# Edge stages of a four-layer graph kernel: ten numbers per quad read in one load of bytes

## The reference

```python
# L0, two layers          # L1                              # L3, two layers
msg = x[src] * ew         messages = x[col] @ W_msg + b     h_ref = x[src] - 2 * dot * rel[etype]
agg = segment_sum(msg, dst)  msg_sum = segment_sum(messages, row)   out = segment_sum(h_ref, tgt)
```

## Time and profile before

| | |
|---|---|
| runs | 4398.54, 4406.31, 4406.6 us; median 4406.31 us |
| span of the profiled execution | 4783.9 us |
| TensorE clock granted, mean | 0.898 |
| PE busy | 3733.3 us (78%), 18662 matmuls |
| DVE busy | 3413.8 us (71%) |
| ACT busy | 2211.2 us (46%) |
| POOL busy | 2954.6 us (62%) |

### The profile page before, as it was taken

One profiled execution on the slowest core, in us unless ns is written; L12 is line 12 of the kernel. 1 busy time (PEld: TensorE's weight loads), 2 busy tenths in 40 slices (PEclk: granted clock), 3 DMA queues, 4 the chain that ended last, 5 costly groups with the idle time before them and its releaser, 6 DMA issues.

```text
span 4783.9 us, 90087 instructions
## 1 busy us (share of the span) xinstructions
PE 3733.3 (78%) x18662; PEld 2281.7 (48%) x18662; DVE 3413.8 (71%) x13249; ACT 2211.2 (46%) x4608; POOL 2954.6 (62%) x3411
## 2 busy tenths in 40 slices
PE   2155799998778999777899999995678774778776
PEld 1012344477523455422598888894224442234443
DVE  5338965355665577743498988897877888768898
ACT  0000046733225688633366666664145652256666
POOL 4650355366566699866466666664665776656787
PEclk6556899999889999889899999997899997999999
DMA  3340157777524788534555555552456773467776
GB/s 88 99 74 6 53 173 222 251 230 232 168 86 159 246 259 271 175 124 130 170 166 161 167 162 161 161 168 66 122 180 227 235 234 113 147 194 246 226 238 194
DMA packets 536159, 810.98 MB, mean 170 GB/s; under 512 B 129245, under 2 KB 184005, under 8 KB 535709
## 3 DMA queue, kind: packets, MB, share of 16 engines
q1 hardware_dynamic: 318844, 532.13, 35.3%
q10 hardware_dynamic: 162769, 169.41, 10.5%
q0 software_dynamic: 54096, 104.47, 8.0%
HBM read 493.49 MB, written 311.41 MB: 168 GB/s over the span
## 4 chain that ended last, share of the span: by engine, by line
PE 47%; DVE 19%; issue 14%; DVEq 6%; POOL 6%; DMA 3%; another core or an unknown queue 2%; ACT 1%; POOLq 0%; ACTq 0%; SPq 0%; PEldq 0%
PE ps L1554 18%; DVEq L68 5%; DVE stat L1122 4%; PE ps L1719 4%; PE ps L1700 4%; PE ps L1701 4%; DVE hit L1071 3%; PE ps L1487 3%; POOL got L719 2%; PE ps L1679 2%; POOL x2T L734 2%; PE ps L1710 2%; PE ps L1680 2%; DVE mv L1128 2%
## 5 line engine op out<-in xcount | busy, mean ns | idle before, releaser
L754 POOL TENSOR_TENSOR rstd<-vare,neg_half 128x4 f32<-128x4 f32 x686 | 710.3, 1035 | 430.6 <-DVE vare L1135 429.6
L1554 PE MATMUL ps<-hit,got 128*128 128x512 bf16 x1172 | 492.5, 420 | 381.7 <-issue 155.9
L1316 ACT ACTIVATE evac<-ps 128x512 f32<-128x512 f32 x392 | 233.4, 595 | 861.8 <-PE ps L1554 625.3
L719 POOL DMA_INDIRECT got<-nodes_l,sorted_by_dst x392 | 398.2, 1016 | 239.5 <-PE ps L1554 109.8
L1554 PE MATMUL ps<-hit,tail 128*128 128x512 bf16 x1172 | 490.2, 418 | 22.8 <-issue 20.8
L1554 PE MATMUL ps<-hit,rest 128*128 128x512 bf16 x1172 | 491.9, 420 | 20.2 <-issue 18.9
L1163 DVE TENSOR_TENSOR nT<-sums,ps 128x512 f32<-128x512 f32 x392 | 268.9, 686 | 270.8 <-PE ps L1599 100.3
L1301 ACT ACTIVATE ps<-zeros 128x512 f32<-128x512 f32 x588 | 344.3, 598 | 195.0 <-DVEq L428 170.1
L1554 PEld LDWEIGHTS ps<-hit,got 128*128 x1172 | 121.8, 104 | 649.3 <-issue 566.0
L719 POOL DMA_INDIRECT got_pair<-in_x,sorted_by_dst x196 | 203.5, 1038 | 363.5 <-DVEq L428 190.1
L669 POOL DMA_INDIRECT records_by_src<-record,place_src x196 | 201.1, 1026 | 162.0 <-PE ps L1587 90.6
(11 more groups left out here) (276 smaller groups left out, 10298.4 us busy)
## 6 DMA issues: line engine op xcount, KB each, us to landing
nodes_l<-xout SPq DMA_DIRECT2D x196, 256.0 KB
xin<-nodes_l SPq DMA_DIRECT2D x196, 256.0 KB
sums<-sums_l SPq DMA_DIRECT2D x196, 256.0 KB
sums_l0a<-evac_pair ACTq DMA_DIRECT2D x98, 256.0 KB
sums_l<-evac_pair ACTq DMA_DIRECT2D x98, 256.0 KB
sums<-sums_l0a SPq DMA_DIRECT2D x98, 256.0 KB
sums_l0b<-evac ACTq DMA_DIRECT2D x98, 256.0 KB
sums<-sums_l0b SPq DMA_DIRECT2D x98, 256.0 KB
```

What stands on the lines that cost most here:

```text
L719: pool.indirect_dma_start(out=BUFFERS[name].got[0][:, k % RING, :], out_offset=None, in_=table, in_offset=bass.IndirectOffsetOnAxis(ap=sor ...
L754: pool.tensor_tensor(rstd[:, n, at, :], vare[:, n, at, :], neg_half[:, :], ALU.pow)\
L1316: act.activation(w.evac[h][:, slot, :], ps[:, BANKS * h + g % BANKS, :], ACT.Copy).then_inc(s["out"].sem, 1)
L1554: last = pe.matmul(into, part.rearrange("p a d -> p (a d)"), w.hit[:, i % w.hits, :], start=False, stop=False, skip_group_check=True)
```

## The change

The two tables become one of bytes, with rows of 16: bytes 0 to 3 hold the slots, 4 to 7 the banks, 8 the batches to wait for and 9 the banks to wait for. PE loads ten bytes of one row at each boundary.

```diff
-        step_tab = {n: sb(f"step_tab_{n}", [1, FOURS, 2 * K], I32) for n in ("dst", "src")}
-        wait_tab = {n: sb(f"wait_tab_{n}", [1, FOURS, 2], I32) for n in ("dst", "src")}
+        step_tab = {n: sb(f"step_tab_{n}", [1, FOURS, 4 * K], U8) for n in ("dst", "src")}
...
-                dve.tensor_scalar(wait_tab[name][:, :, 1], tab_i[:, 1, K - 1:STEPS + 3:K], 1, GROUPS, ALU.add, ALU.min)
-                dve.drain()
-                dve.tensor_scalar(wait_tab[name][:, :, 0], tab_i[:, 3, K - 1:STEPS + 3:K], 1, BATCHES, ALU.add, ALU.min)
+                dve.tensor_scalar(step_tab[name][:, :, 2 * K + 1], tab_i[:, 1, K - 1:STEPS + 3:K], 1, GROUPS, ALU.add, ALU.min)
+                dve.drain()
+                dve.tensor_scalar(step_tab[name][:, :, 2 * K], tab_i[:, 3, K - 1:STEPS + 3:K], 1, BATCHES, ALU.add, ALU.min)
...
-                dve.memset(wait_tab[name][:, :, :], 0)
...
-                def numbers(table, q, lo, hi):
+                def numbers(q):
 
                     return nc.values_load_multi_w_load_instructions(
-                        table[by][0:1, q, lo:hi], engines=[PE_ENGINE], min_val=0, max_val=TILES,
-                        skip_runtime_bounds_check_because=IN_RANGE)[1]
-
-                def waits_of(q):
-
-                    return nc.values_load_multi_w_load_instructions(
-                        wait_tab[by][0:1, q:q + 2, :].rearrange("a q f -> a (q f)"), engines=[PE_ENGINE], min_val=0, max_val=TILES,
+                        step_tab[by][0:1, q, 0:2 * K + 2], engines=[PE_ENGINE], min_val=0, max_val=TILES,
                         skip_runtime_bounds_check_because=IN_RANGE)[1]
...
-                waits = waits_of(0)
-                of = numbers(step_tab, 0, 0, 2 * K)
+                of = numbers(0)
                 for q in range(FOURS):
-                    ready, clear = waits[2 * (q % 2):2 * (q % 2) + 2]
+                    ready, clear = of[2 * K:2 * K + 2]
...
                     if q + 1 < FOURS:
-                        of = numbers(step_tab, q + 1, 0, 2 * K)
-                        if q % 2:
-                            waits = waits_of(q + 1)
+                        of = numbers(q + 1)
```

More of the change, by code:

```diff
@@ L10 @@
 U16 = mybir.dt.uint16
+U8 = mybir.dt.uint8
 ALU = mybir.AluOpType
```

## The result

The changed kernel takes 4899.73 us (median of four, 4896.23 to 4900.48), the kernel before beside it 4402.43 us. The ratio is 1.113, 95% interval 1.1115 to 1.1145: **497 us slower**, where 11 us faster was forecast.

What follows compares the result with a forecast made beforehand. In four edge stages no engine is full; the loop with PE's late queue bounds them. Second load saves 40.4 us, ten bytes lose 22.4; 18.0 times 0.62 takes 11.2 us off 4406.3: 4395 us, range 4355 to 4420.

Steps and rivals of the forecast that it cites:

- What bounds the stage: In l0b, l1, l3a, l3b no engine is full; the loop bounds them, and PE's queue is late at quad boundaries.
- The boundaries that start late: In the four stages, 92 odd boundaries start 0.59 us late and 80 even ones 0.22 us, with no wait behind it.
- Its check: First matmuls of steps in the four stages have 155.9 us unexplained idle before them; the 172 boundaries take about half.
- Term 1: Second load removed at 92 exposed odd boundaries: 34.0 us at 0.37 us each, plus 6.4 for longer loads, together 40.4 us.
- Term 2: First load of ten bytes priced by registers at 721 ns, 0.13 us more at 172 late boundaries: 22.4 us lost.
- A fixed number of exposed boundaries: Only 172 boundaries of the four stages pay for load time; the rest are hidden or wait for data, losing nothing.
- l0a worth nothing: In l0a twice the matmuls hide the loads, so its 37 removed second loads gain nothing; 14 us if they didn't.
- The share 0.62: Share of any microsecond of PE in the four stages that reaches the end, the mean of 61.3%, 72.8%, 58.1% and 56.3%.
- The 378 us between span and times: Profiled execution is 378 us longer than timed runs; a rival blamed recording: nothing to save, 4403 us, chance 0.16.
- The one on the slower side: Rival: bytes cost more, 97 ns for each number, the boundary load takes 1046 ns, 23 us slower, 4430 us; chance 0.12.
- The flat price: Rival: ten bytes at a boundary cost what eight words cost, 592 ns; 25 us saved, 4381 us; chance 0.12.
- the price by bytes: Rival: the boundary load is priced by bytes, 334 ns, so late starts vanish; 48.5 us saved, 4358 us; chance 0.22.

Runs made afterwards that it cites:

- e1: The kernel before, without any edit, recorded a second time: 4401.45 us, ratio 0.999, span 4397.9 us.
- e7: Changed kernel with one word table, a row for two quads, loading twelve words at odd boundaries, eight at even: 4376.7 us, 0.9944 of the kernel before.
- e5: Changed kernel with its table in 32-bit words and twelve words asked for per load: 4391.04 us, ratio 0.9979 to the kernel before.
- e2: Changed kernel with its table in 32-bit words, ten words per load in place of ten bytes: 4417.14 us, ratio 1.0029 to the kernel before.
- e9: Changed kernel loading the whole row of sixteen bytes in place of ten: 5648.16 us beside 4810.2 us for the kernel before, ratio 1.1742.
- e11: The kernel of e7 unchanged, timed again: 4781.72 us beside 4810.2 us for the kernel before, ratio 0.9945.
- e3: Kernel before with its step numbers as bytes, eight a load, wait values still four words in their own load: 4806.87 us, ratio 1.0915.
- e8: Changed kernel with its byte row read as four words and unpacked by shifts and masks in registers: 4580.47 us, ratio 1.0403 to the kernel before.

## Why the prediction was wrong, point by point

- **What bounds the stage: right.** The loop, and PE's queue in it, as the views showed. The reading that a nanosecond of load is a nanosecond of lateness, less some 0.37 us, holds at the boundary shown of the changed kernel: a load of 2.80 us, 2.41 us late.
- **The boundaries that start late: the counts right for the loads of before, the sizes too small.** In the second recording it is 86 odd and 84 even ones that are late directly behind their load, against the 92 and 80 counted. But they are 1.04 and 0.48 us late in the mean, where the prediction took 0.59 and 0.22 from one boundary of each kind. Its check showed this: 172 boundaries at those sizes made only half of the idle time. In the changed kernel all 292 are late, and 70 of the 73 of `l0a`.
- **Term 1, the second load: its size in the end is not shown.** It keeps the queue longer than the 0.37 us taken: 439 ns in the mean in e1's trace, and 58 ns ahead of it. But e7, which takes it away for 258 ns more in the other load (850 in place of 592), shortens the edge stages by 1.5 us only.
- **Term 2, ten bytes at 721 ns: wrong, and this is the step that failed.** They take 2383 ns at the least. I saw that the two rows for loads allow two readings, a price for each register and a price for each 16 bytes, and took the first, which was an assumption of mine: the rows fitted both alike. No run shows a load of 721 ns, or 64.5 ns for a register. Words in full fours follow the second (334, 592 and 852 ns in the median for four, eight and twelve, e5); ten words take 1070 ns at the least (e2), where neither reading has more than 850. Both readings also assumed that a byte is at worst something like a word. The text said that no row sets a bound for that, and then set one, 1.5 times a word's register. Had the bound been 258 ns a byte, the dearest piece that the same text had worked out, the range would have reached 76 + 10 x 258 = 2.66 us. That is near what was measured, and the one end that mattered.
- **The price alone doesn't make the size.** With 2383 ns in place of 721 the prediction's own sum gives 172 x 1.79 = 308 us lost and 40 gained, times 0.62 is 166 us. Measured are 497. The other 331 us are the next three points: boundaries that were hidden or waited for data become late too, `l0a` loses, and more of it arrives.
- **A fixed number of exposed boundaries: wrong at this size.** The 120 that the prediction left out, as hidden or waiting for data, become late as well once each load takes 1.8 us more.
- **l0a worth nothing: wrong at this size.** Its matmuls hide 0.98 us of loads (592 + 58 + 334 ns: 10 of its 73 boundaries are late in e1's trace), not 2.4 (70 of 73 in the changed kernel). It lost 112 us, the most of the five.
- **The share 0.62: too low at this size.** 0.62 was a share of the lateness at 172 boundaries; in three kernels 0.82 to 0.84 of all of the queue's added time arrives. For small doses it is no constant: e2 has 104 us more of queue time and loses 13 us, and e5 has 23 us more and gains 9. Part of this is the stretch between `l1` and `l3a`, which is 13 and 12 us shorter in these two than in e1; the edge stages alone are 42 and 9 us longer.
- **The 378 us between span and times: misread.** It is no cost of recording (e1); the recording shows the slower condition of e9 to e11. Against the 4395 us this did no harm, since the 11 us were taken off the timed runs.
- **The rivals.** The one on the slower side came nearest. It had each byte priced by itself and decided at a load of 827 ns, but its price, 97 ns for a number and 1046 ns for the load, was too low by more than half: 233 ns for a byte (e3) and 2383 ns were measured. It was given 0.12. The rows had words alone (592 ns for eight), and the change was about bytes. The flat price (592 ns) and the price by bytes (334 ns) fail at the same 2383 ns.

**What stays open.** Why the stretch between `l1` and `l3a` takes 994 us in some kernels and 979 to 983 in others, which is most of e7's gain, and for e5 as much as it gains. Why loads of bytes are mostly recorded 0.4 us longer than their shortest. And what share of the 497 us the granted clock of 0.50 makes: 141 us appear in the distances between matmuls inside the quads, but some of that hides loads, and no run separates the two.

## What to carry to other kernels

The loads of registers here took 334, 592 and 852 ns in the median for four, eight and twelve 32-bit words, but at the least 1070 ns for ten words and 2383 ns for ten bytes. By these figures a table for them is kept in 32-bit words, and four, eight or twelve of them are asked for, even if some aren't used. When a change puts an operation into a form that no row of the trace shows (another type, another count), take as its upper bound the price of doing it piece by piece, with the dearest piece that the rows allow: here 2.66 us, where 2.38 us was measured, and the mild factor on the nearest row gave 1.05. When an operation gets several times longer, count anew which places it exposes: here 170 of 292 boundaries before, 273 after. Look for a gain in the stage that was edited: a total that moves the right way may have moved elsewhere, as 15.4 of e7's 19.0 us did. And count an instruction of a busy queue by its distance to the next, not by its recorded duration: in e8 one recorded with 32 ns kept the queue for at least 89.

## What the runs showed of the hardware

- A load of registers on PE takes 334, 592 and 852 ns for 4, 8 and 12 words (medians), at the least 1070 ns for 10 words, 1917 and 2383 ns for 8 and 10 bytes, 2382 ns for ten 16-bit numbers, and for 16 bytes 3787 ns (e9).
- A register instruction on PE is mostly recorded with 32 to 55 ns and cost 86 ns each in e8; between the end of one instruction of this queue and the start of the next lie at least 57 ns there.
- At one boundary of the changed kernel, after 2.63 us without a matmul start, the first three distances were 0.22 us and the next ones 0.41 to 0.43 us, at a granted clock of 0.50 in 1394.20 to 1397.60; behind 1397.60, 4 us after the restart, the granted clock was 1.00 again.
- The same kernel takes 4402 us in one series of runs and 4810 us in another, and 4784 us in the first recording, where single register instructions on PE of up to 1393 ns were recorded; in the recording of 4398 us they take at most 84 ns. What makes the difference stays open.
